# A second attention layer that loads the transposed context stored by the first and scales its columns

## The reference, cut to what matters

```python
def rmsnorm(x, g):
    return x * rsqrt(mean(x * x, axis=-1, keepdims=True) + 1e-6) * g

# first layer, cross-attention: keys and values of the context as it is
K, V = context @ ca_wk + ca_bk, context @ ca_wv + ca_bv
# second layer: keys and values of the normalised context, masked
c = rmsnorm(context, g_c)
Q, K, V = rmsnorm(query, g_q) @ Wq, c @ Wk, c @ Wv
scores = where(mask, Q @ K.T * hd ** -0.5, -inf)
out = rmsnorm(query + softmax(scores) @ V @ Wo, g_out)
```

## Time and profile before

| | us |
|---|---|
| median of 3 runs | 621.56 (620.89 to 623.77) |
| the profiled execution | 622.76 |
| its span (first to last instruction) | 621.0 |
| mean granted TensorE clock | 0.916 |

### The profile page before, as it was taken

How to read it: one execution, slowest core, us unless ns; L and a number is a source line. 1 busy time by engine, 2 the same in 40 slices (tenths; PEclk the granted TensorE clock), 3 DMA queues, 4 the chain that set the end, 5 groups by cost and what they waited for, 6 DMA issues and landing times.

```text
span 621.0 us, 17918 instructions
## 1 busy us (share of the span) xinstructions
PE 529.7 (85%) x6536; PEld 385.6 (62%) x6536; DVE 424.9 (68%) x814; ACT 366.8 (59%) x718; POOL 214.6 (35%) x361
## 2 busy tenths in 40 slices
PE   6867749998998999898779994799989988999985
PEld 4654526766766676676657773467656665667763
DVE  1868857776876779787353125878959895986863
ACT  2635327775776777577424432386757665776663
POOL 6485322130321225372123001535625371721011
PEclk9968758998999899999959997699979997999998
DMA  5326468656375373627502220356362743346100
GB/s 159 96 71 186 129 202 223 196 171 172 115 184 172 100 216 131 174 108 195 153 0 68 68 69 12 99 158 211 134 163 110 178 145 102 121 104 190 36 3 16
DMA packets 41101, 79.77 MB, mean 128 GB/s; under 512 B 9326, under 2 KB 19246, under 8 KB 41054
## 3 DMA queue, kind: packets, MB, share of 16 engines
q1 hardware_dynamic: 41054, 79.16, 43.8%
HBM read 58.95 MB, written 20.13 MB: 127 GB/s over the span
## 4 chain that ended last, share of the span: by engine, by line
PE 53%; issue 12%; DVE 11%; POOL 7%; ACT 7%; SPq 6%; DMA 3%; ACTq 1%; POOLq 1%; DVEq 0%
PE bank L430 9%; PE bank L408 9%; PE bank L396 8%; PE bank L1266 5%; PE bank L358 4%; PE bank L364 4%; PE bank L1255 4%; PE bank L352 3%; DVE mx L592 3%; ACT scratch L545 2%; ACT qfix L522 2%; POOL key_rs L738 1%; PE bank L370 1%; POOL kparts L708 1%; DVE qfix L584 1%
## 5 line engine op out<-in xcount | busy, mean ns | idle before, releaser
L592 DVE TENSOR_REDUCE mx<-bank 112x1 f32<-112x500 f32 x384 | 245.3, 673 | 61.8 <-PE bank L396 58.5
L545 ACT ACTIVATE scratch<-bank 125x448 f32<-125x448 f32 x384 | 203.6, 548 | 120.2 <-PE bank L408 118.3
L396 PE MATMUL bank<-krep,qfix 96*112 96x500 bf16 (+1 forms) x384 | 155.6, 415 | 6.7 <-DVE mx L592 2.7
L408 PEld LDWEIGHTS bank<-qfix,krep 99*128 99x128 bf16 (+1 forms) x1536 | 109.8, 102 | 73.4 <-issue 24.8
L408 PE MATMUL bank<-qfix,krep 99*128 99x112 bf16 (+1 forms) x1536 | 142.1, 217 | 14.3 <-ACT qfix L522 8.8
L430 PE MATMUL bank<-scratch,v 125*32 125x112 f32 x3072 | 95.2, 262 | 3.8 <-ACT scratch L545 3.8
L430 PEld LDWEIGHTS bank<-scratch,v 125*32 125x32 f32 x3072 | 70.0, 109 | 14.4 <-ACT scratch L545 5.8
L396 PEld LDWEIGHTS bank<-krep,qfix 96*112 96x112 bf16 (+1 forms) x384 | 52.1, 137 | 29.6 <-issue 18.0
L708 POOL TENSOR_TENSOR kparts<-k_rest,kparts 128x500 bf16<-128x500 f32 x48 | 54.6, 1146 | 31.4 <-ACT kparts L529 31.1
L719 POOL TENSOR_TENSOR oT<-comb,rec 128x56 f32 (+1 forms) x32 | 9.9, 311 | 155.5 <-DVE rec L614 155.5
L1266 PEld LDWEIGHTS bank<-scratch 128*112 128x112 f32 x256 | 33.5, 185 | 15.7 <-issue 10.5
(11 more groups left out here) (170 smaller groups left out, 734.8 us busy)
## 6 DMA issues: line engine op xcount, KB each, us to landing
krep<-k_scratch SPq DMA_DIRECT2D x192, 187.5 KB, 3.9
k_scratch<-kparts SPq DMA_DIRECT2D x16, 1125.0 KB, 4.6
ctx_tile<-in_ctx SPq DMA_DIRECT2D x16, 750.0 KB
scratch<-in_L_xattn_e_w SPq DMA_DIRECT2D x16, 256.0 KB, 3.1
Q<-q_scratch SPq DMA_DIRECT2D x12, 168.0 KB, 3.3
q_scratch<-scratch SPq DMA_DIRECT2D x6, 168.0 KB, 3.0
Q<-q_scratch SPq DMA_DIRECT2D x12, 56.0 KB, 2.3
k_rest<-in_selq SPq DMA_DIRECT2D x1, 576.0 KB, 8.9
```

Of the source, the lines that this page charges most:

```text
L396: nc.tensor.matmul(row_bank(v, c, lead)[0:PQ, 0:KB], qfix[0:KR[l], slot, p * PQ:(p + 1) * PQ], krep[0:KR[l], slot, p, n * KB:(n + 1) * KB] ...
L408: ins = nc.tensor.matmul(SCORES[c % 2][:, p * PQ:(p + 1) * PQ], krep[0:KS[l], slot, p, c * KP:c * KP + 128], qfix[0:KS[l], slot, p * PQ:(p ...
L545: nc.scalar.activation(P[:, p_slot(s_, slot), :], SCORES[slot % 2][0:KP, 0:UQ], ACT.Exp, scale=SCALE).then_inc(z["exp_ok"], 1)
L592: nc.vector.tensor_reduce(mx[:, par, c // NKB, c % NKB:c % NKB + 1], row_bank(v, c, lead)[0:PQ, 0:KB], AX.X, ALU.max).then_inc(z["row_max" ...
```

## The change

- The first layer's `ctxT` of every batch is stored in DRAM (`sp_ct_store`, new `ct_scratch`, 768 KB a batch) right after the T that makes it.
- The second layer has no T. `sp_ct_load` loads `ctxT` from there, and POOL's `pool_scale` multiplies it by `rs_row`, a tile of 128 partitions that all hold the batch's 1500 key scales. K waits for that product (`ctx_ok`) and not for T.
- The scales come from the same squares and sums as before (now with a slot for each batch in `key_ss` and `key_rs`). `pool_key_scales` makes them, for batch 0 and 1 at the first layer's third pass (j == 2), for batches 2 to 7 in one go behind the experts' squares. `sp_scales_write` stores a batch's 125 x 12 scales as one row in DRAM (`rs_scratch`), and `sp_scales_load` loads that row into all 128 partitions of `rs_row`, which has one buffer. `rs_row`, `v_all` and `weights` share one tile, `early`.
- In SyncE's body `scaled_context` does these loads: for batch 2j + 3 behind the first replication of batch 2j + 2, for batch 2j + 4 at the body's end. For the second layer's batches 0 and 1, the scale write stands between the two loads.
- During the experts SP loads the six context tiles between the expert weights; behind the last weights it writes six scale rows and loads the row of batch 2, and then comes the query.
- In `STEP_ITEMS` K keeps its slots; T goes to slots 4, 6 and 8 of a body's second and fourth half batch, one batch further ahead, V to slot 11 and to slots 0 and 2 of the next half batch. T of batch 2 moves ahead of the first layer's loop. PE and ACT run two passes looped and two written out.

```diff
+        ct_scratch = nc.dram_tensor("ct_scratch", (B, 128, SK), F32, kind="Internal").ap()
+        rs_scratch = nc.dram_tensor("rs_scratch", (B, SK), F32, kind="Internal").ap()
...
-        key_ss = sb("key_ss", [KP, KC])
-        key_rs = sb("key_rs", [KP, KC])
+        key_ss = sb("key_ss", [KP, B, KC])
+        key_rs = sb("key_rs", [KP, B, KC])
...
-        v_all = sb("v_all", [S, B, 128])
         WT = 7 * S + 128 - S
-        weights = sb("weights", [128, 2, WT])
+        early = sb("early", [128, 2 * WT + B * 128])
+        weights = early[:, 0:2 * WT].rearrange("p (r n) -> p r n", r=2)
+        v_all = early[0:S, 2 * WT:].rearrange("p (b d) -> p b d", b=B)
+        rs_row = early[:, 0:SK]
...
-            {0: [("T", 2, 0)], 1: [("T", 2, 1)], 2: [("T", 2, 2)], 4: [("K", 2, 0)],
...
+            {4: [("K", 2, 0)], 6: [("K", 2, 1)], 8: [("K", 2, 2)], 10: [("M", 1)], 11: [("V", 1, 0)]},
+            {0: [("V", 1, 1)], 2: [("V", 1, 2)], 4: [("T", 3, 0)], 5: [("D", -1)], 6: [("T", 3, 1)],
...
-                    if layer > 1 or (isinstance(n, int) and n >= U):
+                    if layer > 1 or (isinstance(n, int) and n >= U) or (it[0] == "T" and layer == 1):
...
                 if i == 0:
-                    if l == 0:
-
-                        pe.wait_ge(z[f"ctx_in{par}"], 16 * (n // 2 + 1) if isinstance(n, int) else (n - par) * 8 + 16)
-                    else:
-                        pe.wait_ge(z["ctx_ok"], n + 1)
+                    pe.wait_ge(z[f"ctx_in{par}"], 16 * (n // 2 + 1) if isinstance(n, int) else (n - par) * 8 + 16)
...
             if kind == "K":
-                pe.wait_ge(z["t_ok"], 3 * n + i + 1)
+                if l == 0:
+                    pe.wait_ge(z["t_ok"], 3 * n + i + 1)
+                else:
+                    pe.wait_ge(z["ctx_ok"], n + 1)
...
+                if i == 0 and not (isinstance(n, int) and n < 2):
+                    act.wait_ge(z[f"ct_w{par}"], 16 * (n // 2) if isinstance(n, int) else (n - par) * 8)
...
+        def squares_here(l, j, s_):
+            return l == 0 and isinstance(j, int) and j == 2 and s_ in (0, 2)
...
+        def pool_squares(pool, n, par):
+            z = L[1]
+            pool.wait_ge(z[f"ctx_in{par}"], 16 * (n // 2 + 1))
+            if n:
+                pool.wait_ge(z["ss_ok"], n)
             tile = ctx_tile[:, par, :, :]
             nc.gpsimd.tensor_tensor(sq[:, :, :], tile, tile, ALU.mult).then_inc(z["sq_ok"], 1)
 
-        def pool_norm(pool, l, n, par):
-
-            z = L[l]
-            link = Chain(pool, z["pool_n"], POOL_N * n)
-            tile = ctx_tile[:, par, :, :]
-            pool.wait_ge(z["ss_ok"], n + 1)
...
-            nc.gpsimd.tensor_tensor(tile, tile, wide(key_rs[:, :], 128, 2), ALU.mult).then_inc(z["ctx_ok"], 1)
+        def pool_key_scales(pool, lo, hi, k):
+            z, m = L[1], hi - lo
+            link = Chain(pool, z["pool_n"], 3 * k)
+            rs = key_rs[:, lo:hi, :]
+            pool.wait_ge(z["ss_ok"], hi)
+            link(nc.gpsimd.tensor_tensor(rs, key_ss[:, lo:hi, :], wide(inv_d[0:KP, :], m, 1), ALU.mult))
+            link(nc.gpsimd.tensor_tensor(rs, rs, wide(rms_eps[0:KP, :], m, 1), ALU.add))
+            link(nc.gpsimd.tensor_tensor(rs, rs, wide(neghalf[0:KP, :], m, 1), ALU.pow))
+            nc.gpsimd.tensor_tensor(rs, rs, mask_col[:, lo:hi, :], ALU.mult).then_inc(z["rs_ok"], 1)
+        def pool_scale(pool, n, par):
+            z = L[1]
+            pool.wait_ge(z[f"ct_in{par}"], 16 * (n // 2 + 1) if isinstance(n, int) else (n - par) * 8 + 16)
+            pool.wait_ge(z["rs_in"], 16 * n + 16)
+            nc.gpsimd.tensor_tensor(ctxT[:, par, :], ctxT[:, par, :], rs_row, ALU.mult).then_inc(z["ctx_ok"], 1)
 
         def pool_attend(pool, link, l):
...
             pool_mparts(pool, l, 0, 0)
+            if l == 1:
+                pool_scale(pool, 2, 0)
 
             def body(j):
                 last = isinstance(j, int) and j == 3
...
-                    layer_n, m = where(l, 2 * j + 3 + s_ // 2)
-                    if s_ in (0, 2) and norm_here(layer_n, m):
-                        pool_squares(pool, layer_n, m, s_ // 2 ^ 1)
-                    if s_ in (1, 3) and norm_here(layer_n, m):
-                        pool_norm(pool, layer_n, m, s_ // 2 ^ 1)
+                    if squares_here(l, j, s_):
+                        pool_squares(pool, s_ // 2, s_ // 2)
+                    if s_ in (1, 3) and squares_here(l, j, s_ - 1):
+                        pool_key_scales(pool, s_ // 2, s_ // 2 + 1, s_ // 2)
...
+                    layer_n, m = where(l, 2 * j + 3 + s_ // 2)
+                    if s_ in (1, 3) and layer_n == 1 and not (l == 0 and m == 2):
+                        pool_scale(pool, m, s_ // 2 ^ 1)
...
+        def sp_ct_store(sp, n, par):
+            z = L[0]
+            sp.wait_ge(z["t_ok"], 3 * n + 3)
+            dst = ct_scratch[n] if isinstance(n, int) else \
+                ct_scratch[bass.ds(n, 1)].rearrange("o p n -> (o p) n")
+            sp.dma_start(dst, ctxT[:, par, :]).then_inc(z[f"ct_w{par}"], 16)
+        def sp_ct_load(sp, n, par):
+            z = L[1]
+            if isinstance(n, int) and n < 2:
+                sp.wait_ge(L[0][f"ct_w{par}"], 16 * (B // 2))
+                sp.wait_ge(L[0]["v_ps"], 3 * (B - 2 + n) + 3)
+            else:
+                sp.wait_ge(z["v_ps"], 3 * n - 3)
+            src = ct_scratch[n] if isinstance(n, int) else \
+                ct_scratch[bass.ds(n, 1)].rearrange("o p n -> (o p) n")
+            sp.dma_start(ctxT[:, par, :], src).then_inc(z[f"ct_in{par}"], 16)
+        def sp_scales_write(sp, n, k):
+            sp.wait_ge(L[1]["rs_ok"], k + 1)
+            sp.dma_start(rs_scratch[n].rearrange("(c p) -> p c", p=KP), key_rs[:, n, :],
+                         allow_slow_non_contiguous=True).then_inc(s["rs_written"], 16)
+        def sp_scales_load(sp, n):
+            z = L[1]
+            sp.wait_ge(s["rs_written"], 16 * n + 16 if isinstance(n, int) and n < 2 else 16 * B)
+            if not (isinstance(n, int) and n == 0):
+                sp.wait_ge(z["ctx_ok"], n)
+            src = rs_scratch[n:n + 1] if isinstance(n, int) else rs_scratch[bass.ds(n, 1)]
+            sp.dma_start(rs_row, src.to_broadcast([128, SK])).then_inc(z["rs_in"], 16)
         def sp_attend(sp, l):
...
+            def scaled_context(n, par):
+                layer, b = where(l, n)
+                if layer != 1:
+                    return
+                sp_ct_load(sp, b, par)
+                if l == 0 and b < 2:
+                    sp_scales_write(sp, b, b)
+                if not (l == 0 and b == 2):
+                    sp_scales_load(sp, b)
 
             def body(j):
                 sp_krep(sp, l, 4 * j + 3, 3, 2 * j + 1, 1)
...
                 v = n * HALVES
-                context(2 * j + 4, 0)
+                if layer == 0:
+                    context(2 * j + 4, 0)
+                    sp_ct_store(sp, n, 0)
                 sp_kwrite(sp, layer, n, 0)
                 sp_krep(sp, layer, v, 0, n, 0)
+                scaled_context(2 * j + 3, 1)
                 sp_krep(sp, layer, v + 1, 1, n, 0)
-                context(2 * j + 5, 1)
+                if layer == 0:
+                    context(2 * j + 5, 1)
+                    sp_ct_store(sp, n + 1, 1)
                 sp_kwrite(sp, layer, n + 1, 1)
                 sp_krep(sp, layer, v + 2, 2, n + 1, 1)
+                scaled_context(2 * j + 4, 0)
...
-            with sp.Fori(0, E // 2 - 1) as i:
-                for r in range(2):
-                    sp.wait_ge(s["y_part"], 8 * i + 4 * r + 4)
-                    sp_expert(sp, 2 * i + 2 + r, r)
+            for n in range(2, B):
+                if n >= 4:
+                    e = n - 4
+                    sp.wait_ge(s["y_part"], 4 * e + 4)
+                    sp_expert(sp, e + 2, e % 2)
+                sp.wait_ge(L[1]["sq_ok"], n - 1)
+                sp_ctx(sp, 1, n, n % 2)
+            for e in range(B - 4, E - 2):
+                sp.wait_ge(s["y_part"], 4 * e + 4)
+                sp_expert(sp, e + 2, e % 2)
+            for n in range(2, B):
+                sp_scales_write(sp, n, 2)
+            sp_scales_load(sp, 2)
...
+            def third_batch(i):
+                if i == 0:
+                    pe.wait_ge(s["q_sb"], 2)
+                    pe.wait_ge(L[0]["qfix_ok"], 1)
+                pe_item(pe, ("T", 2, i, 0, 0), i, ("T", 2, 0, 0, 0) if i == 2 else None)
...
-            with dve.Fori(0, E // 2 - 1) as i:
-                for r in range(2):
-                    add_expert(2 * i + r, r).then_inc(s["y_used"], 1)
+            for e in range(E - 2):
+                add_expert(e, e % 2).then_inc(s["y_used"], 1)
+                dve_ss(dve, 1, 2 + e)
...
-            pool_squares(pool, 1, 2, 0)
-            pool_norm(pool, 1, 2, 0)
+            for n in range(2, B):
+                pool_squares(pool, n, n % 2)
+            pool_key_scales(pool, 2, B, 2)```

```

(1 more changed line is left out.)

56 lines of the change are left out of this document (25 added, 31 removed), and 10 rows, old and new, of the table STEP_ITEMS.

## The result

The changed kernel takes 746.8 us (742.3 to 750.5), the kernel before 621.2: 1.201 times as long, 95% interval 1.196 to 1.205. The prediction was 713 with a range of 655 to 800: slower, as forecast, by 126 us instead of 92. The profiled execution took 750.5 with a span of 748.7; it is the slowest of the four. One execution of a later version ("Everything off the path") took 1611.7 us and is left out of that version's median.

What follows compares the result with a forecast made beforehand. TensorE was taken to bound the loops, and a serial chain through DRAM to replace it. 621.0 + 34.1 + 1.5 + 30.3 + 23.0 + 2.5 = 712.4 of span, so 713 us, range 655 to 800.

Steps and rivals of the forecast that it cites:

- the 34.1 before it: First layer's tail: the second layer's second K at 316.3 against 284.75, +31.6, and the restart, together +34.1 us.
- The term for squares: First layer's tail: batch 1's squares on GpSimd delay the row-maximum parts, so TensorE waits 7.0 us.
- the −2.2 for T ahead of the loop: First layer: batch 2's transposes move ahead of the loop into TensorE's idle time, so everything behind comes 2.2 us earlier.
- Tail: End of first layer: scale writes of batches 0 and 1 stand in the chain; first K at 275.2, second at 316.3.
- Gate: Behind the experts: six scale writes of 6.0 us each precede the query; +32.5, less 2.2 for T, +30.3 us.
- Experts: Expert stage: late scales hold a root 0.8 us, and weights sharing DMA with tile loads cost 0.7: +1.5 us.
- Loop: Second layer: a serial chain of 30.65 us plus slower clock makes 33.1 a batch against 28.5; five intervals, +23.0 us.
- the restart 2.5: TensorE after each pause before K: it runs at the lower clock for a while, costing 2.5 us.
- that of the two loads: Second layer's chain: issue, fixed cost and transfer of the ctxT and scale-row loads, estimated at 5.8 us in all.
- Hidden loads: Rival: SyncE issues loads early enough, chain stays below 25 us, six writes finish before 385.6; 597 us, chance 0.06.
- Slow broadcast row: Rival: the scale row's load into 128 partitions runs at 35 GB/s; 790 to 850 us, chance 0.10.
- Dearer 4-byte writes: Rival: a 4-byte write costs 60 ns, 12 us a scale write, eight writes: +96, 809 us, chance 0.08.

Runs made afterwards that it cites:

- Everything off the path: Changed kernel with squares and element-wise scale-row writes moved into the first layer's loop, no reloads during the experts, loads ahead of the key write: 674.2 us.
- the last experiment: Against the version with all three ideas and no reloads: batches 0 and 1 normalised in place and transposed by TensorE, no element-wise scale writes: 616.7 us.
- the version with all three ideas and no reloads: Against Everything off the path: scales of batches 2 to 7 transposed, written as 72 rows; row loaded early, context behind key write; sums later: 625.2 us.

## Why the prediction was right, and where it was short

The sign and the mechanism held at each of the five places; the sizes by place, as times of the span, predicted and measured (each measured figure carries what was late before it, and is from the slowest execution, so the rows sum to 36 where the medians differ by 34):

| | predicted | measured | short by, at this place |
|---|---|---|---|
| last K of the first layer | 229.0 | 240.0 | 11.0 |
| first K of the second layer | 275.2 | 291.2 | 5.0 |
| second K | 316.3 | 334.3 | 2.0 |
| query write behind the experts (417.1 and the 34.1 before it) | 451.2 | 470.8 | 1.5 |
| third K (406.1 + 34.1 + 1.5 + 30.3) | 472.0 | 490.2 | −1.3 |
| last K (and 5 × 33.1) | 637.5 | 673.0 | 17.3 |
| end | 712.4 | 748.7 | 0.8 |

- **Last K of the first layer.** The term for squares was counted once and happens twice. I priced batch 1's (TensorE would wait 7.0; it waited 6.8) and passed over batch 0's, which stands a batch earlier in the same way and makes a wait of 5.3 us and, with the slower clock behind it, a K interval of 32.7 instead of 25.1: 7.6. TensorE's waits for the parts:

```profile
220.29 0.53 PE L374 MATMUL bank<-identb,mparts 112*4 112x112 bf16 x4 [5.34 <-POOL mparts L706]
...
255.02 0.53 PE L374 MATMUL bank<-identb,mparts 112*4 112x112 bf16 x4 [6.78 <-POOL mparts L706]
```

  And the −2.2 for T ahead of the loop didn't show: the first K of the loop came between 96.6 and 99.4 us in the kernels with it, 97.4 before. Nor did the loop get shorter by it: from its first K to the last of the layer it is 134.4 us in the version of the last experiment, 133.8 before.
- **Tail.** The chain ran as written: key write, replications, row write, row load, product. In order of time:

```profile
261.35 5.65 DMA k_scratch<-kparts
...
271.49 10.24 DMA rs_scratch<-key_rs
281.75 5.81 DMA early<-rs_scratch
287.69 3.35 POOL ctxT L753
```

  The write took 10.2 us (for the next batch 9.0) where I had 8.9 with its issue, the row 5.8 where I had 3.9, the product 3.35 where I had 2.8. From the parts to the key write I had 5.3, for which no row stood (4.1 in the kernel before, 239.42 to 243.52); it was 6.3.
- **Gate.** From the scales to the query write I had 38.3 us; it was 36.4. A write took 5.9 us, and I had 6.0, but not by my working: a packet is under way for 29 ns and not 20, and 7.5 are under way at a time and not five. The two errors cancelled, which was luck. Whether the writes lay beside one another on different engines or several packets on one, the trace doesn't tell. The Trainium skill's rule that I weighed (page "DMA: Bandwidth & Descriptors", section "Rules for kernel authors": a last dimension that isn't contiguous becomes one descriptor per element) is what the trace shows, 1500 packets for 6 KB. By the 10.5 ns a packet of the Trainium skill (the same page, section "Bandwidth") the six writes come to 6 × 300 × 10.5 ns = 18.9 us, an estimate; they took 35.6.
- **Experts.** I had +1.5 for the stage; from its first product to the third norm it took 69.8 us instead of 63.8. The scales held the first root of the norm back by 1.1 us (0.8 forecast): its input was there at 433.6, the root began at 434.8. The rest is the expert weights, behind the tile loads on the same engines, which I had put at 0.7:

```profile
PE bank L1337 <- DMA scratch<-in_L_xattn_e_w: 4.5, 4, 1.5
```

  This excess was hidden by the gate's shortfall in the table. In the three versions without those loads the stage takes 62.9 to 64.6 us, about the old length.
- **Loop.** The K interval was 36.6 us against 33.1, the step that cost most: 17.3 in five. The links, for one batch:

```profile
542.68 0.42 SPq L802 DMA_DIRECT2D k_scratch<-kparts  x1
547.40 5.38 SPq L815 DMA_DIRECT2D krep<-k_scratch  x6
552.97 0.67 SPq L820 DMA_DIRECT2D krep<-mask_scratch  x1
553.94 0.35 SPq L856 DMA_DIRECT2D ctxT<-ct_scratch  x1
554.53 0.33 SPq L871 DMA_DIRECT2D early<-rs_scratch  x1
```

```profile
560.88 3.34 POOL L753 TENSOR_TENSOR ctxT<-ctxT,early 128x1500 f32<-128x1500 f32 x1 [10.66 <-DMA early<-rs_scratch]
```

  On the mean of the five intervals: K to key write 14.8 (I had 12.0 and the restart 2.5), to the replication 4.7 (4.8), to the context load 5.7 (5.25), to the product 7.9 (5.8), product and start of K 3.4 (2.8). So the term that was sized too small is that of the two loads, 2.1 of the 3.5 us a batch: the product starts 5.7 to 9.0 us after the issue of the row's load. I had taken the time of a transfer that stands alone, while replications are issued right behind these; that this is the reason was not run by itself.
- **The rivals.** Hidden loads: no, but the condition I gave for it was the right one: with the row early and the context behind the key write, the first two loop batches have their product done 24.9 and 23.8 us after the K before it; K isn't held, and the interval falls to 26.6. Slow broadcast row: no, 768 KB to 128 partitions landed in a median of 6.2 us. Dearer 4-byte writes: no, 5.9 us a write at the gate, 9.0 and 10.2 in the tail beside a context load, and not 12 of data alone.

About four fifths of the rise came back in runs: 54 us with two loads in another place, 38 with larger packets, 8 with later squares, each alone, 100 of 126. That they add up was not run; the version with all three ideas and no reloads came to 625. Of the remainder the traces say where most of it lies. None of the three edits takes the loads of batches 0 and 1 out of the serial way through the first layer's tail. The second K of the second layer was 49.5 us late in the changed kernel (334.3 against 284.75); by the traces the later squares gave 13 back there and the packets 13, and the last version, which has no such way in the tail, comes at 285.1; that leaves some 23. The reloads during the experts are some 5 us more. The T path and the stores are not in it, since the last version has both and keeps the first layer's beat.

## What to carry to other kernels

A step that is taken off a busy engine and given to DMA pays only if the transfer's issue doesn't stand behind a wait that itself depends on the step before: write the loop as a chain from one use to the next and compare its length with the engine's own beat, here 30 against 25. Move the transfer to the first point at which its buffer is free, but not ahead of one that others wait for; a small reordering (one load half a batch early, one behind the key write) was worth 54 us. And turn a column of numbers into rows on an engine, here one transpose, before it goes to DRAM.

## What the runs showed of the hardware

- Six DRAM writes of 1500 pieces of 4 bytes took 35.6 us, 5.9 each (29 ns of packet time a piece); one of them in the first layer's tail, with a 768 KB load beside it, 9.0 or 10.2. In 48-byte pieces the six took 4.9, as 72 rows of 500 bytes 2.4 in one version and 4.1 in the last.
- They also delay others: beside such a write six replications landed after a median of 7.7 us instead of 3.6.
- GpSimd's power over 72 values per partition took 11.88 us, 2.27 over twelve and 0.55 over one: linear, 0.16 us a value, as extrapolated.
